# Context features of two blocks in one operation each, in a Trainium2 kernel of softmax attention and linear attention

## The reference

```python
# layer 0: softmax attention, 16 heads of 32
Q, K, V = x @ Wq.T + bq, ctx @ Wk.T + bk, ctx @ Wv.T + bv
x = layernorm(softmax(Q K^T / sqrt(32)) V @ Wo.T + bo + x) * gamma0 + beta0
# layer 1: linear attention
Q_phi, K_phi = elu(x), elu(ctx)
KV = einsum('bnd,bne->bde', K_phi, ctx)
Z  = 1 / (einsum('bnd,bd->bn', Q_phi, K_phi.sum(axis=1)) + 1e-6)
x = layernorm(x + einsum('bnd,bde->bne', Q_phi, KV) * Z[..., None]) * gamma1 + beta1
```

## Time and profile before

| | |
|---|---|
| median of three runs | 1516.23 us (1515.08 to 1519.13) |
| the profiled execution's own time | 1515.14 us |
| its span, first to last instruction | 1513.8 us |
| mean granted TensorE clock | 0.995 |
| TensorE busy | 1472.3 us, 97% |
| VectorE busy | 1246.4 us, 82% |
| ScalarE busy | 869.4 us, 57% |
| GpSimd busy | 1242.4 us, 82% |

### The profile page before, as it was taken

The page is one execution under the profiler, slowest core; times in us unless marked ns, Lnnn a source line. Parts: engine busy times, 40 slices in busy tenths (PEclk is TensorE's granted clock), DMA queues, the critical chain, the costliest instruction groups (busy, mean ns, idle before and its releaser), DMA issues.

```text
span 1513.8 us, 30356 instructions
## 1 busy us (share of the span) xinstructions
PE 1472.3 (97%) x10584; PEld 1037.9 (69%) x10584; DVE 1246.4 (82%) x2447; ACT 869.4 (57%) x1723; POOL 1242.4 (82%) x1153
## 2 busy tenths in 40 slices
PE   8999999999999999999999999999999999999896
PEld 6767767676766767667676767666767668766554
DVE  6697888878888889887879888998688878798865
ACT  3465655556555556665556555665566655666653
POOL 0487787768899998877799999887789989898975
PEclk9999999999999999999999999999999999999998
DMA  7754254443325235344344425435152342430000
GB/s 224 202 158 124 77 156 129 144 113 114 108 68 170 77 108 158 97 119 129 101 117 116 117 72 170 133 86 161 62 143 93 119 127 92 119 94 21 14 29 35
DMA packets 159575, 170.14 MB, mean 112 GB/s; under 512 B 20288, under 2 KB 122048, under 8 KB 159424
## 3 DMA queue, kind: packets, MB, share of 16 engines
q1 hardware_dynamic: 157696, 167.16, 37.7%
q10 hardware_dynamic: 1728, 1.05, 0.2%
HBM read 125.97 MB, written 42.21 MB: 111 GB/s over the span
## 4 chain that ended last, share of the span: by engine, by line
PE 79%; POOL 6%; DVE 4%; issue 4%; DMA 3%; ACT 2%; SPq 1%; POOLq 0%; ACTq 0%; DVEq 0%
PE score L472 14%; PE scoreT L486 13%; PE acc L504 13%; PE misc L554 7%; PE misc L543 7%; PE misc L591 6%; PE misc L566 6%; PE misc L530 6%; PE misc L583 4%; POOL pair_sum L1068 3%; PE acc L520 2%; DVE maxes L803 1%; DVE pair_sum L843 1%; DMA q_stack<-q_dram 1%; POOL pair_sum L1077 1%
## 5 line engine op out<-in xcount | busy, mean ns | idle before, releaser
L658 ACT ACTIVATE p_ring<-scoreT 128x512 f32<-128x512 f32 x1024 | 596.3, 595 | 507.0 <-PE scoreT L486 498.9
L1068 POOL TENSOR_TENSOR pair_sum<-p_ring 128x512 f32<-128x512 f32 x504 | 664.6, 1327 | 163.6 <-ACT p_ring L658 97.0
L803 DVE TENSOR_REDUCE maxes<-score 128x1 f32<-128x512 f32 x1024 | 675.1, 678 | 134.5 <-PE score L472 129.2
L472 PE MATMUL score<-k_stack,q_stack 96*128 96x512 f32 x1024 | 597.5, 585 | 7.1 <-DVE maxes L803 3.1
L486 PEld LDWEIGHTS scoreT<-q_stack,k_stack 104*128 104x128 f32 x2048 | 386.2, 190 | 157.0 <-ACT p_ring L658 84.2
L486 PE MATMUL scoreT<-q_stack,k_stack 104*128 104x256 f32 x2048 | 419.2, 286 | 8.2 <-ACT p_ring L658 5.9
L472 PEld LDWEIGHTS score<-k_stack,q_stack 96*128 96x128 f32 x1024 | 192.6, 188 | 164.0 <-issue 104.2
L1077 POOL TENSOR_TENSOR pair_sum<-pair_sum 128x512 f32<-128x512 f32 x189 | 248.2, 1313 | 0.0
L504 PE MATMUL acc<-p_ring,v_sb 128*32 128x256 f32 x4096 | 247.6, 382 | 0.0
L843 DVE TENSOR_TENSOR pair_sum<-pair_sum 128x512 f32<-128x512 f32 x189 | 211.2, 1118 | 5.7 <-POOL pair_sum L1068 5.6
L504 PEld LDWEIGHTS acc<-p_ring,v_sb 128*32 128x32 f32 x4096 | 120.0, 109 | 83.8 <-issue 0.8
(11 more groups left out here) (112 smaller groups left out, 1397.5 us busy)
## 6 DMA issues: line engine op xcount, KB each, us to landing
xT_sb<-xT_in SPq DMA_DIRECT2D x63, 512.0 KB, 3.9
q_stack<-q_dram SPq DMA_DIRECT2D x189, 128.0 KB, 2.6
k_stack<-k_dram SPq DMA_DIRECT2D x93, 256.0 KB, 4.7
ctx_nat<-ctx_in SPq DMA_DIRECT2D x32, 256.0 KB, 4.8
q_dram<-q_high SPq DMA_DIRECT2D x63, 128.0 KB, 1.7
q_dram<-q_low SPq DMA_DIRECT2D x63, 128.0 KB, 1.9
k_dram<-k_high SPq DMA_DIRECT2D x31, 256.0 KB, 2.0
k_dram<-k_low SPq DMA_DIRECT2D x31, 256.0 KB, 2.4
```

Of the source, the lines that this page charges most:

```text
L472: pe.matmul(score[k % 3][:], q_stack[0:SPLIT, unit % NQ, j, t * P:(t + 1) * P], k_stack[0:SPLIT, group_of[unit] % 2 * QUAD + j, h * HALF:( ...
L658: act.activation(p_ring[:, n % NP, h * HALF:(h + 1) * HALF], scoreT[k % 2][:], ACT.Exp, scale=SCALE).then_inc(A["exped"], 1)
L803: dve.reduce_max(maxes[:, unit % 2, t, j, h:h + 1], score[k % 3][:], AX.X).then_inc(V["maxed"], 1)
L1068: pool.tensor_tensor(pair_sum[:, place_of_pair(pair), cols], p_ring[:, (n - 1) % NP, cols], p_ring[:, n % NP, cols], ALU.add).then_inc(L[" ...
```

## The change

The features are made for two blocks, t and t+1, in one operation on ScalarE (relu, exp) and one on VectorE, 256 columns wide; `f_sb` holds one pair instead of two blocks, `fphi_sb` two pairs instead of three blocks. A pair that opens at tick k is made on ScalarE at k-3, on VectorE at k-2, and summed on GpSimd at k-1 by the same additions as before, two in one tick. The sum matmuls stay as they are, each waits for its pair. The planner's reservations follow. Also: `ones` is 32 columns wide and the column totals are four matmuls of 32 output rows; the small columns of the norms are packed into one tensor.

```diff
-    NPHI = 3
+    NPHI = 2
+    PAIRS = KT // 2
-        fphi_sb = sb("fphi_sb", [P, NPHI, P])
+        fphi_sb = sb("fphi_sb", [P, NPHI, 2, P])
-        ones = sb("ones", [P, P])
+        ones = sb("ones", [P, DK])
...
-                        take("ACT", k - 4, 5)
-                        take("DVE", k - 3, 5)
-                        take("POOL", k - 2, 5)
+                        if pieces[k][1] % 2 == 0:
+                            take("ACT", k - 3, 9)
+                            take("DVE", k - 2, 8)
+                            take("POOL", k - 1, 10)
...
-                pe.wait_ge(V["f_phi"], piece + 1)
-                pe.matmul(bank_of("S", i)[:], fphi_sb[:, piece % NPHI, :], ctx_nat[:, t, :],
+                pe.wait_ge(V["f_phi"], piece // 2 + 1)
+                pe.matmul(bank_of("S", i)[:], fphi_sb[:, piece // 2 % NPHI, t % 2, :], ctx_nat[:, t, :],
...
-                pe.matmul(bank_of("N", b)[:], ones[:], phi_total[:], start=True, stop=True).then_inc(T["k_totalled"], 1)
+                for j in range(QUAD):
+                    mm = pe.matmul(bank_of("N", b)[j * DK:(j + 1) * DK, :], ones[:], phi_total[:], start=True, stop=True,
+                                   tile_position=(0, j * DK), skip_group_check=True)
+                mm.then_inc(T["k_totalled"], 1)
...
-                if piece >= 2:
-                    act.wait_ge(V["f_phi"], piece - 1)
-                act.activation(f_sb[:, piece % 2, :], ctx_nat[:, t, d * P:(d + 1) * P], ACT.Relu,
+                if pair >= 1:
+                    act.wait_ge(V["f_phi"], pair)
+                f = f_sb[:]
+                act.activation(f, ctx_nat[:, 2 * q:2 * q + 2, d * P:(d + 1) * P], ACT.Relu,
                                scale=-1.0).then_inc(A["f_below"], 1)
...
-                piece = sum_piece(k + 4)
-                if piece is not None:
-                    context_features(piece)
+                pair_of_features = sum_pair(k + 3)
+                if pair_of_features is not None:
+                    context_features(pair_of_features)
...
-                if piece >= NPHI:
-                    dve.wait_ge(T["kv_piece"], piece - NPHI + 1)
-                    i, before = divmod(piece - NPHI, KT)
-                    dve.wait_ge(L["totalled"], (KT - 1) * i + max(before, 1))
+                if pair >= NPHI:
+                    dve.wait_ge(T["kv_piece"], 2 * (pair - NPHI + 1))
+                    i, before = divmod(pair - NPHI, PAIRS)
+                    dve.wait_ge(L["totalled"], (KT - 1) * i + 2 * before + 1)
                 dve.scalar_tensor_tensor(
-                    out=fphi_sb[:, piece % NPHI, :], in0=f_sb[:, piece % 2, :], scalar=-1.0,
-                    in1=ctx_nat[:, t, d * P:(d + 1) * P], op0=ALU.add,
+                    out=fphi_sb[:, pair % NPHI, :, :], in0=f_sb[:], scalar=-1.0,
+                    in1=ctx_nat[:, 2 * q:2 * q + 2, d * P:(d + 1) * P], op0=ALU.add,
                     op1=ALU.max).then_inc(V["f_phi"], 1)
...
-                piece = sum_piece(k + 3)
+                pair_of_features = sum_pair(k + 2)
...
+                first, second = (fphi_sb[:, pair % NPHI, t, :] for t in range(2))
+                if q == 0:
                     if i >= G:
                         pool.wait_ge(V["dotted"], KT * (i // G))
+                    pool.tensor_tensor(whole, first, second, ALU.add).then_inc(L["totalled"], 1)
                 else:
+                    pool.wait_ge(L["totalled"], (KT - 1) * i + 2 * q - 1)
+                    pool.tensor_tensor(whole, whole, first, ALU.add).then_inc(L["totalled"], 1)
+                    pool.wait_ge(L["totalled"], (KT - 1) * i + 2 * q)
+                    pool.tensor_tensor(whole, whole, second, ALU.add).then_inc(L["totalled"], 1)
...
-                piece = sum_piece(k + 2)
+                pair_of_features = sum_pair(k + 1)
```

More of the change, by code:

```diff
@@ L126, in build @@
         max_turned = sb("max_turned", [P, 2, DK])
[L127 to L133, removed]
+        norm_parts = sb("norm_parts", [P, NX + 4, 7])
+        sums, neg_mean, centre_at, var, var_eps, rstd, shift = (norm_parts[:, :, n:n + 1] for n in range(7))
         minus_half = sb("minus_half", [P, 1])
@@ L448, in chain_freed, with sum_pair @@
                     "B": V["bias_folded"]}[kind], i + 1
-        def sum_piece(k):
+        def sum_pair(k):
             chain, piece = pieces.get(k, (None, 0))
-            return KT * chain[1] + piece if chain and chain[0] == "S" else None
+            return PAIRS * chain[1] + piece // 2 if chain and chain[0] == "S" and piece % 2 == 0 else None
         def tensor_program():
@@ L510, in visit @@
                         for j in range(QUAD):
-                            mm = pe.matmul(acc[j * DK:(j + 1) * DK, CH:2 * CH], ones[:, 0:DK],
+                            mm = pe.matmul(acc[j * DK:(j + 1) * DK, CH:2 * CH], ones[:],
                                            p_ring[:, n % NP, j * CH:(j + 1) * CH], start=False,
@@ L636, in tensor_program @@
             for _ in range(8):
-                pe.matmul(misc[1][:, 0:P], ones[:], ident[:], start=True, stop=True)
+                pe.matmul(misc[1][0:DK, 0:P], ones[:], ident[:], start=True, stop=True)
             for k in range(FIRST, LAST):
@@ L731, in keep_ksum, with context_features @@
                 act.activation(phi_total[:], bank_of("N", b)[:], ACT.Copy).then_inc(A["ksum_kept"], 1)
[L733 to L736, removed]
-                if piece >= 2:
-                    act.wait_ge(V["f_phi"], piece - 1)
-                act.activation(f_sb[:, piece % 2, :], ctx_nat[:, t, d * P:(d + 1) * P], ACT.Relu,
+            def context_features(pair):
+                d, q = pair // PAIRS % G, pair % PAIRS
+                if pair % (G * PAIRS) == 0:
+                    act.wait_ge(M["ctx"], 16 * KT * (pair // (G * PAIRS) + 1))
+                if pair >= 1:
+                    act.wait_ge(V["f_phi"], pair)
+                f = f_sb[:]
+                act.activation(f, ctx_nat[:, 2 * q:2 * q + 2, d * P:(d + 1) * P], ACT.Relu,
                                scale=-1.0).then_inc(A["f_below"], 1)
-                act.wait_ge(A["f_below"], piece + 1)
-                act.activation(f_sb[:, piece % 2, :], f_sb[:, piece % 2, :], ACT.Exp,
-                               scale=-1.0).then_inc(A["f_grown"], 1)
+                act.wait_ge(A["f_below"], pair + 1)
+                act.activation(f, f, ACT.Exp, scale=-1.0).then_inc(A["f_grown"], 1)
             def keep_kv(i):
@@ L977, in keep_kv_low, with context_features @@
                                   ALU.subtract).then_inc(V["kv_low_kept"], 1)
[L979 to L985 removed]
+            def context_features(pair):
+                d, q = pair // PAIRS % G, pair % PAIRS
+                dve.wait_ge(A["f_grown"], pair + 1)
+                if pair >= NPHI:
+                    dve.wait_ge(T["kv_piece"], 2 * (pair - NPHI + 1))
+                    i, before = divmod(pair - NPHI, PAIRS)
+                    dve.wait_ge(L["totalled"], (KT - 1) * i + 2 * before + 1)
                 dve.scalar_tensor_tensor(
[L987 to L988 removed]
+                    out=fphi_sb[:, pair % NPHI, :, :], in0=f_sb[:], scalar=-1.0,
+                    in1=ctx_nat[:, 2 * q:2 * q + 2, d * P:(d + 1) * P], op0=ALU.add,
                     op1=ALU.max).then_inc(V["f_phi"], 1)
@@ L1146, in gpsimd_program @@
             for k in range(FIRST, LAST):
-                piece = sum_piece(k + 2)
-                if piece is not None:
-                    add_features(piece)
+                pair_of_features = sum_pair(k + 1)
+                if pair_of_features is not None:
+                    add_features(pair_of_features)
                 if k in when["bias"]:
```

13 lines of the change are left out of this document (3 added, 10 removed).

## The result

The changed kernel takes 1531.34 us (median of four runs, 1527.44 to 1533.63), the kernel before 1517.68 in the same comparison: a ratio of 1.0094, 95% interval 1.0073 to 1.0114. The forecast was 1527.5, slower, by stalls in front of eight sum matmuls.

The account below looks back on a forecast made before the run. TensorE, busy 1472.3 of 1513.8 us, was taken to bound the kernel. Terms 12.8 plus 0.7 plus 1 minus 2.6 gave +12 us on 1515.14, so 1527.5 us; range 1516 to 1536.

Parts of the forecast that it names:

- TensorE sets the end, and the saved work is off its path: Whole kernel: 32 us saved on VectorE and 26 on ScalarE are worth nothing unless they end a TensorE wait.
- batch 3: TensorE's waits for VectorE at 1351.51, 1360.62 and near 1338 us: relief of 2.2 us, bounds 0 and 3.
- The lost tick of lead puts the pair behind the high addition at eight ticks: Ticks 60, 124, 204, 460, 476, 716, 732, 972: VectorE's pair operation comes late, stalling TensorE 1.6 us each, 12.8 together.
- The upper bound: At tick 460, GpSimd's two small additions also delay the pair, out near 627.0: a stall of 2.0 us at most.
- Ticks 452 and 708: Pairs there have no high addition before them but meet a GpSimd p addition: 0.35 us each.
- Pairs behind a visit: 0: Pairs just behind a visit have 1.5 us more time, so no stall was counted.
- worse: Rival: late pairs delay GpSimd, so pairs behind visits and in close chains stall too; +24 us and more, 1540; chance 0.10.
- the close chains: Eight chains with pieces at consecutive ticks: about 1 to 2 us margin; 1 us loss over all, bounds 0 and 4.
- The totals cost nothing: Column totals: four matmuls of 32 output columns side by side overlap and add nothing; 12 us if they did not.
- Every transfer unchanged: Planner: new reservations touch no later booking, so TensorE's order and every transfer stay unchanged.
- It doesn't show: Rival: less loaded VectorE and GpSimd run further ahead, so the stall is gone; -2 to +4 us, some 1516; chance 0.22.
- Faster: Rival: relief of VectorE ends its waits in batch 3, the start and beside spaced chains; 1509 to 1511 us; chance 0.08.

Follow-up runs that it names:

- the last two runs: Changed kernel with pairs one tick earlier, totals as one matmul, small additions apart: ratio 1.0013; the same with the very first pair one tick later: 0.9994.

## Why the prediction was right, step by step

- *TensorE sets the end, and the saved work is off its path.* Right. What was saved gave TensorE 1.7 us in batch 3 and hardly more (2.2 forecast). The third wait there, at tick 972, is hidden behind the late pair. The wait of 1.14 us at 77.2 went from tick 50, and ticks 51 and 52 grew by 1.4 instead; ticks 41 to 52 came out 0.3 shorter in all, where 0.4 was counted, too little to tell. The saving itself was put too high: 32 and 26 us were forecast, and VectorE and ScalarE are each busy 17.6 less. The durations of the feature operations fell by 37.7 and 25.9, but a part of these had overlapped other operations, and VectorE's high additions took 11.3 us more (211.2 to 222.5).
- *The lost tick of lead puts the pair behind the high addition at eight ticks.* Right in place, order and offsets. The size is 10.8 us (1.12 to 1.72 each) where 12.8 was summed at 1.6 each, inside the bounds of 1.0 and 2.0. The upper bound has a slip: a pair out near 627.0, where TensorE needs it at 624.60, is a stall of 2.4 and not 2.0. At tick 476, where 1.5 to 2.0 was said, it was 1.24. That GpSimd's two small additions are a part of it is shown by the run with one column: half of the sum went.
- *Ticks 452 and 708.* 0.65 and 0.67 where 0.35 was said.
- *Pairs behind a visit: 0.* Wrong at one. Tick 968, just behind a visit, grew by 2.1 us, in spite of the 1.5 us of extra time that was counted for such places:

```profile
1367.49 1.74 DVE L843 TENSOR_TENSOR pair_sum<-pair_sum 128x512 f32<-128x512 f32 x1 [2.07 <-POOL pair_sum L1068]
...
1370.70 1.12 PE L588 MATMUL misc<-ctx_nat,fphi_sb 128*128 128x512 f32 x2 [1.83 <-DVE fphi_sb L986]
```

  Timeline of VectorE and TensorE, changed kernel: VectorE stood idle for 2.07 us before the high addition, until GpSimd's p addition was done. Two things load GpSimd here. Four bias additions of 1.3 us stand on ticks 957 to 961, in the kernel before too, where tick 968 was not late. And the small additions now come two at a time ahead of the p addition: put behind it, or taken apart with the lead given back, they left tick 968 as before; with the lead back alone it grew by 1.0, and with additions of one column by 1.4. So the small additions are needed for this stall; that the bias additions are needed too I only argue, no run took them away. This is the rival "worse" at one place; in the close chains nothing grew (1 us had been allowed).
- *The totals cost nothing.* Wrong, by 1.4 us. The ratio of the acc rows that I leaned on is an average over sixteen matmuls in a row; a lone group of four does not reach it.
- *Every transfer unchanged.* Their order is unchanged, their moments are not. The transfer queue of the kernel before, then of the changed one, ahead of tick 448:

```profile
598.53 0.34 SPq L1273 DMA_DIRECT2D res_out<-tiles  x1
...
599.45 1.06 SPq L1192 DMA_DIRECT2D ctxT_sb<-ctxT_in  x2
602.85 1.28 SPq L1217 DMA_DIRECT2D q_stack<-q_dram  x3
```

```profile
604.05 0.35 SPq L1273 DMA_DIRECT2D res_out<-tiles  x1
...
604.97 1.06 SPq L1192 DMA_DIRECT2D ctxT_sb<-ctxT_in  x2
606.89 1.63 SPq L1217 DMA_DIRECT2D q_stack<-q_dram  x3
```

  The store waits for a GpSimd result that now stands behind two small additions. It holds the queue, so the large ctxT transfers start 1.9 us ahead of the queries instead of 3.4, and score 448 waited 1.45 us for these. The gap was 1.9 to 2.3 us in five more of the runs with two additions in one tick, where tick 447 grew by 0.7 to 1.4. With the additions last in their tick it was 4.4, with additions of one column 3.2, and the tick didn't grow. With the additions back on their ticks it was 3.0, and the tick still grew by 0.9 and by 0.3 in the last two runs, so the gap is not all of it.

  Tick 895 has another chain behind it. ScalarE waits there for the landing of a store of keys, VectorE's copy of the keys' low parts (L896) and its high addition come after it, and the visit's last matmuls wait for that. ScalarE's line before, then ScalarE's and TensorE's in the changed kernel:

```profile
1246.63 0.69 ACT L679 ACTIVATE k_high<-misc,bias_cols 128x512 fp32r<-128x512 f32 x1 [2.03 <-DMA k_dram<-k_low]
```

```profile
1261.41 0.69 ACT L679 ACTIVATE k_high<-misc,bias_cols 128x512 fp32r<-128x512 f32 x1 [3.06 <-DMA k_dram<-k_low]
...
1263.63 0.64 PE L517 MATMUL acc<-pair_sum,ones 128*32 128x256 f32 x8 [1.40 <-DVE pair_sum L843]
```

  The store is issued 5.12 us ahead of that tick in every run. It took 5.50 us to land before, 6.54 in the changed kernel (the tick grew by 1.04) and 7.45 with the small additions apart (it grew by 1.95). The other runs lie on the same line within 0.3 us, but for the one with the high addition a tick later. Why the landing time varies is not shown. The two visits add 2.6 us to the profiled execution, which lies 2.3 us above the median; the other executions have no trace, so whether that is the reason stays open.
- *It doesn't show* fell with the pair at tick 460; GpSimd's low addition did not come earlier. *Faster* needed fewer than two late pairs and there were eight. Engine time did fall, from 84.5 us to 46.8 in L986, and it was not what was short. The rule of the Trainium skill that spoke for it ("VectorE: DVE Perf Modes", "The TRN2 errata") agrees with this fall. At each meeting in the rows above VectorE's operation came out after GpSimd's, by 0.55 or 0.29 us. The exclusive lock of the Trainium skill ("SBUF — State Buffer", "SBUF: two separate sides") agrees with that.

How near the time came is partly luck. 12 us were summed; the medians differ by 13.7, and the two profiled executions, from which the terms can be read, by 18.2 in their ticks. 2.0 us less at the eight ticks and 1 less in the close chains stand against 1.4 in the totals, 0.6 at ticks 452 and 708, 3 in batch 3, 2.6 at the two visits, 0.9 less in gains and 0.9 elsewhere.

The runs also say more than the forecast did. Step by step the ratio went from 1.0094 to 1.0054 with the lead back, 1.0052 with one matmul for the totals, 1.0013 with the small additions apart, and 0.9994 with the first pair late. So two additions in one tick on GpSimd cost about as much as the lost lead. The forecast had them only as the upper part of its stalls, and the shares depend on the order of the steps, since both feed the same stalls.

## What to carry to other kernels

When small steps are merged, the first consumer's need does not move but the merged step is done once, and where it stands in each engine's queue counts for more than what it costs: count the operations that it is now behind, and time them from the rows. Merge on the engines that gain and leave the rest alone: here wide operations were free only with the old lead and with the third engine's additions on their old ticks, and even then they gained nothing that the runs can tell, since the two engines were not the bound. Swapping two operations on a full engine moves the wait to the other one's consumer.

## What the hardware showed beyond that

- A VectorE operation of two SBUF sources, during which a GpSimd operation ended, came out a fixed time after that end, longer with its own width: 0.15 us for 128 columns (88 of 97 cases, kernel before), 0.28 for 256 (44 of 45, changed kernel) and 0.55 to 0.56 for 512 (150 of 164, changed kernel). Where no GpSimd operation ended meanwhile, most took 0.28, 0.41 to 0.43 and 0.68 us.
- Four fp32 matmuls of 32 output columns side by side, alone in their tick, took TensorE 0.34 us longer than one of 128 (1.67 against 1.33), at each of four places, in every profiled execution that has them.
